# A gated recurrence on one core: loads in series, half rows first for two tiles, plain warm-up products, the end in two pieces

## What is computed

```python
for i in range(6):                       # ih: (6, 4000, 256), hh: (6, 256, 256)
    gate = ih[i][token]                  # token: 1024 integers, 49 to 31985
    state = jnp.tanh(state + jnp.matmul(state, hh[i]) * gate)
```

## Time and profile before

| what | value |
|---|---|
| median of 3 runs | 63.14 us (62.12, 63.14, 63.68) |
| profiled execution, own time | 62.04 us |
| its span, first to last instruction | 60.2 us |
| TensorE matmul busy | 52.1 us, 86% |
| VectorE busy | 40.5 us, 67% |
| ScalarE busy | 40.0 us, 66% |
| POOL busy | 34.4 us, 57% |
| DMA moved | 4.46 MB |

### The profile page before, as it was taken

How to read it: one execution, slowest core, us unless ns; L and a number is a source line. 1 busy time by engine, 2 the same in 40 slices (tenths; PEclk the granted TensorE clock), 3 DMA queues, 4 the chain that set the end, 5 groups by cost and what they waited for, 6 DMA issues and landing times.

```text
span 60.2 us, 853 instructions
## 1 busy us (share of the span) xinstructions
PE 52.1 (86%) x273; PEld 43.2 (72%) x273; DVE 40.5 (67%) x60; ACT 40.0 (66%) x69; POOL 34.4 (57%) x34
## 2 busy tenths in 40 slices
PE   0879999995887999999999999999999999999000
PEld 0679888872747689896888887888878888885000
DVE  0319974429589885874977778877779777779900
ACT  0703899503329440979999888998888988852430
POOL 4076076777624990298587876667866668700000
PEclk9999999999999999999999999999999999999975
DMA  0598688898400000000000000000000000032254
GB/s 0 12 321 271 211 280 242 222 303 222 131 16 0 0 0 0 0 0 11 0 0 0 0 0 0 0 0 5 11 5 0 0 0 0 0 144 97 107 195 154
DMA packets 5380, 4.46 MB, mean 74 GB/s; under 512 B 2186, under 2 KB 4746, under 8 KB 5376
## 3 DMA queue, kind: packets, MB, share of 16 engines
q1 hardware_dynamic: 3168, 3.41, 17.7%
q0 software_dynamic: 1152, 0.73, 4.8%
q10 hardware_dynamic: 1056, 0.27, 1.9%
HBM read 8.92 MB, written 1.05 MB: 166 GB/s over the span
## 4 chain that ended last, share of the span: by engine, by line
PE 66%; DMA 12%; issue 5%; DVE 5%; ACT 4%; POOL 3%; DVEq 0%; POOLq 0%
PE prod L443 25%; PE prod L452 12%; PE turned L427 12%; PE prod L400 9%; DMA gate<-gates_dram,row_of 8%; PE turned L465 5%; DMA last_row<-gates_dram 4%; PE turned L409 4%; POOL gate L214 3%; ACT gate L256 2%; DVE prod L349 1%; DVE pre L354 1%; DVE gp L338 1%; ACT s L267 1%; ACT s L282 1%
## 5 line engine op out<-in xcount | busy, mean ns | idle before, releaser
L230 POOL TENSOR_TENSOR sl<-s,sh 128x512 fp32r<-128x512 f32 x12 | 15.5, 1291 | 6.0 <-ACT s L282 6.0
L443 PE MATMUL prod<-sh,wr 128*128 128x512 f32 x64 | 18.8, 415 | 0.0
L400 PE MATMUL prod<-w,s 128*128 128x256 f32 x64 | 15.3, 388 | 1.3 <-ACT s L267 0.6
L349 DVE TENSOR_TENSOR prod<-prod,gate_t 128x512 f32<-128x512 f32 x16 | 11.2, 700 | 6.5 <-PE prod L452 6.5
L400 PEld LDWEIGHTS prod<-w,s 128*128 128x128 f32 x64 | 12.1, 197 | 3.1 <-issue 1.7
L443 PEld LDWEIGHTS prod<-sh,wr 128*128 128x128 f32 x64 | 10.9, 189 | 1.5
L282 ACT ACTIVATE s<-pre 128x512 f32<-128x512 f32 x16 | 9.9, 620 | 2.6 <-DVE pre L354 2.6
L354 DVE TENSOR_TENSOR pre<-prod,s 128x512 f32<-128x512 f32 x16 | 11.1, 693 | 0.6
L214 POOL DMA_INDIRECT gate<-gates_dram,row_of x8 | 8.1, 1010 | 5.6 <-issue 2.0
L452 PE MATMUL prod<-sl,wr 128*128 128x512 f32 x32 | 10.0, 395 | 0.0
L427 PE MATMUL turned<-ident,gate 128*128 128x128 f32 x64 | 9.4, 272 | 0.0
(11 more groups left out here) (20 smaller groups left out, 26.6 us busy)
## 6 DMA issues: line engine op xcount, KB each, us to landing
w<-hh_dram SPq DMA_DIRECT2D x5, 256.0 KB
s<-state_t_dram SPq DMA_DIRECT2D x4, 256.0 KB, 3.3
out_t_dram<-s SPq DMA_DIRECT2D x4, 256.0 KB, 2.0
w<-hh_dram ACTq DMA_DIRECT2D x1, 256.0 KB
gate<-gates_dram,row_of POOLq DMA_INDIRECT x8, 3.2
last_row<-gates_dram ACTq DMA_DIRECT2D x1, 6.0 KB, 2.5
tok<-token_dram SPq DMA_DIRECT2D x1, 4.0 KB, 1.7
```

Source lines behind the costliest of these rows:

```text
L230: nc.gpsimd.tensor_tensor(of_unit(sl[:, l % 2], h, c), of_unit(s, h, c), of_unit(sh[:, l % 2], h, c).bitcast(f32), ALU.subtract).then_inc( ...
L349: nc.vector.tensor_tensor(prod_bank[u][:, :], prod_bank[u][:, :], gate_t[:, u], ALU.mult).then_inc(unit_gated[u], 1)
L400: last = nc.tensor.matmul(prod[q][:, t, :], of_quarter(s, q)[:, c, t * P:(t + 1) * P], w[:, l, c, :], start=c == 0, stop=c == KC - 1)
L443: nc.tensor.matmul(prod_bank[u][:, :], wr[:, l, k, half, c * P:(c + 1) * P], of_unit(sh[:, (l - 1) % 2], h, k), start=half == 0 and k == 0 ...
```

## The change

- SP issues each load only when the one before it has landed: state 2 behind state 1, then state 3, weights 1, 2, 3, 4 and 5 in turn.
- Tiles 0 and 1 are fetched in halves of a row, through a view of the table with twice as many rows (`half_of` is twice the row). The first halves (layers 0 to 2) are gathered first and patched on VectorE; the second halves are gathered behind all other tiles, into space that ScalarE has filled with two more fills. VectorE has one patch fewer.
- The warm-up products are nine plain matmuls of 64 columns on a tile of zeros that VectorE clears, in place of five transposes of the identity.
- `gate_t` has two buffers, by the parity of the layer, and the order of ScalarE's gate copies is written out anew.
- The last tanh and the last store are cut into two pieces of 256 batch columns.

```diff
-WARM_UP = 5
...
-LATE_TILES = [0, 1]
+WARM_UP = 9
+EARLY_TILES = [0, 1]
...
+HALF = LAYERS // 2 * HIDDEN
+EARLY, REST = slice(0, HALF), slice(HALF, 2 * HALF)
...
+ACT_FILLS = [(1, 2, 1), (2, 2, 1), (1, 3, 1), (2, 3, 1), (1, 4, 2), (2, 4, 2), (1, 6, 2), (2, 6, 2), (2, 0, 2)]
+ACT_COUNT = len(ACT_FILLS) + 1
...
+    half_table = table.rearrange("v (h n) -> (v h) n", n=HALF)
...
-        gate_t = sb("gate_t", [P, UNITS, HB], f32)
+        gate_t = sb("gate_t", [P, 2, UNITS, HB], f32)
...
-                sp.wait_ge(state_in[0], 16)
+                sp.wait_ge(state_in[1], 16)
                 load_state(2)
-                sp.wait_ge(w_in[0], 16)
+                sp.wait_ge(state_in[2], 16)
                 load_state(3)
-                sp.wait_ge(state_in[1], 16)
+                sp.wait_ge(state_in[3], 16)
                 load_weights(1)
-                sp.wait_ge(state_in[2], 16)
-                load_weights(2)
-                sp.wait_ge(state_in[3], 16)
-                load_weights(3)
-                for l in range(4, LAYERS):
-                    sp.wait_ge(w_in[l - 3], 16)
+                for l in range(2, LAYERS):
+                    sp.wait_ge(w_in[l - 1], 16)
                     load_weights(l)
                 for h in range(HALVES):
                     for c in range(KC):
                         sp.wait_ge(unit_s[h * KC + c], wide_done(LAYERS - 1))
-                        sp.dma_start(out_v[h, c], of_unit(s, h, c)).then_inc(out_done, 16)
-                sp.wait_ge(out_done, 16 * UNITS)
+                        if h * KC + c < UNITS - 1:
+                            sp.dma_start(out_v[h, c], of_unit(s, h, c)).then_inc(out_done, 16)
+                        else:
+                            sp.dma_start(out_v[h, c, :, 0:QB], of_unit(s, h, c)[:, 0:QB]).then_inc(out_done, 16)
+                            sp.wait_ge(end_s, 1)
+                            sp.dma_start(out_v[h, c, :, QB:HB], of_unit(s, h, c)[:, QB:HB]).then_inc(out_done, 16)
+                sp.wait_ge(out_done, 16 * (UNITS + 1))
...
+                def gather_early(t):
+                    nc.gpsimd.indirect_dma_start(
+                        gate[:, t, EARLY], None, half_table,
+                        bass.IndirectOffsetOnAxis(half_of[:, t:t + 1].bitcast(u32), 0),
+                        bounds_check=last_half_fetched, oob_is_err=False,
+                    ).then_inc(early_in[t], 16)
+                def gather_rest(t):
+                    pool.wait_ge(filled_act, ACT_COUNT)
+                    nc.gpsimd.indirect_dma_start(
+                        gate[:, t, REST], None, half_table,
+                        bass.IndirectOffsetOnAxis(half_of[:, t:t + 1].bitcast(u32), 0),
+                        element_offset=HALF, bounds_check=last_half_fetched, oob_is_err=False,
+                    ).then_inc(gate_in[t], 16)
                 def gather(t):
-                    if t not in LATE_TILES:
-                        pool.wait_ge(filled_dve, fills_of(t, DVE_FILLS))
-                        pool.wait_ge(filled_act, fills_of(t, ACT_FILLS))
+                    pool.wait_ge(filled_dve, fills_of(t, DVE_FILLS))
+                    pool.wait_ge(filled_act, fills_of(t, ACT_FILLS))
...
+                pool.wait_ge(halves_ready, 1)
+                for t in EARLY_TILES:
+                    gather_early(t)
                 pool.wait_ge(rows_ready, 1)
-                for t in range(TILES):
+                for t in range(len(EARLY_TILES), TILES):
                     gather(t)
+                for t in EARLY_TILES:
+                    gather_rest(t)
...
-                    if l > WIDE:
-                        act.wait_ge(unit_gated[u], wide_done(l - 1))
-                    nc.scalar.copy(gate_t[:, u], turned_bank[u][:, :]).then_inc(gates_copied[u], 1)
+                    if l > WIDE + 1:
+                        act.wait_ge(unit_gated[u], wide_done(l - 2))
+                    nc.scalar.copy(gate_t[:, l % 2, u], turned_bank[u][:, :]).then_inc(gates_copied[u], 1)
...
-                    nc.scalar.activation(of_unit(s, h, c), of_unit(pre, h, c), ACT.Tanh).then_inc(unit_s[u], 1)
+                    if (l, u) != (LAYERS - 1, UNITS - 1):
+                        nc.scalar.activation(of_unit(s, h, c), of_unit(pre, h, c), ACT.Tanh).then_inc(unit_s[u], 1)
+                    else:
+                        s_u, pre_u = of_unit(s, h, c), of_unit(pre, h, c)
+                        nc.scalar.activation(s_u[:, 0:QB], pre_u[:, 0:QB], ACT.Tanh).then_inc(unit_s[u], 1)
+                        nc.scalar.activation(s_u[:, QB:HB], pre_u[:, QB:HB], ACT.Tanh).then_inc(end_s, 1)
...
+                nc.scalar.copy(gate[:, 0:len(EARLY_TILES), HALF:HALF + HIDDEN],
+                               spread[1][:, HIDDEN:2 * HIDDEN].unsqueeze(1).to_broadcast([P, len(EARLY_TILES), HIDDEN]),
+                               ).then_inc(filled_act, 1)
...
+                copy_gates(WIDE, 1, 0)
+                for l in range(WIDE, LAYERS - 1):
+                    wide_tanh(l, 0, 0)
+                    copy_gates(l, 1, 1)
+                    wide_tanh(l, 0, 1)
+                    copy_gates(l + 1, 0, 0)
+                    wide_tanh(l, 1, 0)
+                    copy_gates(l + 1, 0, 1)
+                    wide_tanh(l, 1, 1)
+                    copy_gates(l + 1, 1, 0)
+                wide_tanh(LAYERS - 1, 0, 0)
+                copy_gates(LAYERS - 1, 1, 1)
+                wide_tanh(LAYERS - 1, 0, 1)
+                wide_tanh(LAYERS - 1, 1, 0)
+                wide_tanh(LAYERS - 1, 1, 1)
...
+                nc.vector.memset(blank[:, :], 0.0).then_inc(blank_ready, 1)
...
+                nc.vector.tensor_scalar(wrap[:, :], tok_held[:, :], 0.0, 2.0 * VOCAB, ALU.is_lt, ALU.mult).then_inc(index_step, 1)
...
-                nc.vector.tensor_tensor(row_of[:, :], tok_held[:, :], wrap[:, :], ALU.add).then_inc(rows_ready, 1)
+                nc.vector.scalar_tensor_tensor(half_of[:, :], tok_held[:, :], 2.0, wrap[:, :], ALU.mult, ALU.add).then_inc(halves_ready, 1)
+                dve.wait_ge(halves_ready, 1)
+                nc.vector.tensor_scalar(row_of[:, :], half_of[:, :], 0.5, None, ALU.mult).then_inc(rows_ready, 1)
...
-                def patch(i, t, count):
-                    for late in range(t, t + count):
-                        dve.wait_ge(gate_in[late], 16)
-                    nc.vector.copy_predicated(filled(i, t, count),
-                                              is_last[:, t:t + count].unsqueeze(2).to_broadcast([P, count, PIECE * HIDDEN]),
-                                              filling(i, count)).then_inc(patched, 1)
+                def patch(t):
+                    dve.wait_ge(early_in[t], 16)
+                    nc.vector.copy_predicated(gate[:, t, 0:PIECE * HIDDEN], is_last[:, t:t + 1].to_broadcast([P, PIECE * HIDDEN]),
+                                              spread[0]).then_inc(patched, 1)
+                def patch_rest():
+                    dve.wait_ge(filled_act, ACT_COUNT)
+                    tiles = slice(0, len(EARLY_TILES))
+                    nc.vector.copy_predicated(gate[:, tiles, PIECE * HIDDEN:HALF],
+                                              is_last[:, :].unsqueeze(2).to_broadcast([P, len(EARLY_TILES), HIDDEN]),
+                                              spread[1][:, 0:HIDDEN].unsqueeze(1).to_broadcast([P, len(EARLY_TILES), HIDDEN]),
+                                              ).then_inc(patched, 1)
...
-                patch(0, 0, 1)
+                patch(0)
                 for i, t, count in DVE_FILLS[3:]:
                     fill(i, t, count)
-                patch(0, 1, 1)
+                patch(1)
                 gating(0)
                 gating(1)
                 sum_up(0)
-                dve.wait_ge(filled_act, len(ACT_FILLS))
-                patch(1, 0, 2)
+                patch_rest()
                 gating(2)
                 sum_up(1)
                 sum_up(2)
-                patch(2, 0, 2)
...
+                    if h == 0 and l < LAYERS // 2:
+                        pe.wait_ge(patched, len(EARLY_TILES) + 1)
+                    elif h == 0:
+                        for t in EARLY_TILES:
+                            pe.wait_ge(gate_in[t], 16)
...
+                pe.wait_ge(blank_ready, 1)
+                for _ in range(WARM_UP):
+                    nc.tensor.matmul(turned[0][:, 0, 0:P // 2], blank[:, :], blank[:, 0:P // 2], start=True, stop=True)
                 pe.wait_ge(ident_ready, 1)
-                for _ in range(WARM_UP):
-                    nc.tensor.transpose(turned[0][:, 0, 0:P], ident[:, :], ident[:, :])
```

More of the change, by code:

```diff
@@ L83, in recurrent_cells @@
         row_of = sb("row_of", [P, TILES], i32)
-        is_last = sb("is_last", [P, len(LATE_TILES)], i32)
+        half_of = sb("half_of", [P, TILES], i32)
+        is_last = sb("is_last", [P, len(EARLY_TILES)], i32)
+        blank = sb("blank", [P, P], f32)
         last_row = sb("last_row", [P, LAYERS, KC], f32)
```

(24 more changed lines are left out.)

3 lines of the change are left out of this document (removed).

## The result

| | median us | all runs |
|---|---|---|
| before | 62.84 | 62.12 to 63.68 (4 runs) |
| changed | 67.0 | 65.71, 66.25, 67.76, 69.38 |
| ratio | 1.058 | 95% interval 1.034 to 1.083 |

The change makes the kernel slower. The medians lie 4.2 us apart; the ratio is formed from the fast runs alone (65.71 and 66.25 against 62.12 and 62.55), and by these the loss is 3.6 us. The profiled execution of the changed kernel took 69.38 us (span 67.6), and TensorE's clock dipped in it for 3.3 us: its mean clock is 0.971. The runs of 65.71 and 66.25 have a mean clock of 0.99; a dip of that length alone would bring it to 0.974 (an estimate), so they had none like it.

What follows compares the result with a forecast made beforehand. Gathers hold the kernel up to 18.40 us, then TensorE's fixed order; the start of plain(7) is the mark. +0.8 for serial loads and -0.3 at the end make 62.04 into 62.5, plus half the distance to the median: 63.1, range 60.8 to 65.2.

Steps and rivals of the forecast that it cites:

- the second rival: SP's serial loads cost more, 3.15 to 3.34 us each beside gathers: slower, 64.3 to 65.1 us; chance 0.22.
- the price of a load in series: SP's queue: 2.7 us for each of four loads beside gathers, 2.1 for each of the last three.
- C: Average time of SP's seven serial loads, forecast at 2.44 us; break-even against the profiled execution at 2.37.
- its 63.6: Total in us by the skill's rule, which prices a lone load at 2.6; the forecast kept the rows instead.
- The mechanism: ScalarE: tanh(3) stands behind the rounding of weights 5, so the last plain product, plain(7), starts 0.8 us later.
- The formula 62.04 + 7C - 16.6: Total time from the profiled 62.04 us, the delay of plain(7) by seven serial loads, and 0.3 saved at the end.
- The third rival: TensorE's clock falls in the idle time before plain(7), costing 2.5 us: 65.0 us; chance 0.06.
- the hole before plain(7): TensorE standing idle some 2 us before the last plain product, waiting for tanh(3).
- The warm-up: TensorE's head: earlier start worth nothing while serial loads set the mark, at worst costs nothing; 1.3 to 1.5 us possible.
- The end: Last tanh and store cut in two: 0.3 us faster, between 0 and 0.5.
- Gathers: Gathers fall from 4.54 towards 3.2 us, up to 1.3 won at plain(5), then lost at plain(7).
- Half rows and gate buffers: Half-row fetches save 1.9 us on DVE, which does not end last; doubled gate_t removes a nonbinding wait: nothing.

Runs made afterwards that it cites:

- a_oldwarm: The changed kernel with the five transposes of the identity as warm-up again; 67.75 us, ratio 1.086 to the kernel before.
- b_serial: The kernel before with only SP's seven later loads put in series; 68.41 us against 62.24.
- b_warm: The kernel before with only the warm-up changed to nine plain products of zeros; 63.73 us, ratio 1.024.
- b_end: The kernel before with only the last tanh and last store cut in two; 62.9 us, ratio 1.011.
- a_old3: The changed kernel with loads, warm-up and end of before, leaving half rows, fills and gate buffers; 62.33 us against 62.12, ratio 1.006.
- b_warm_ones: The kernel before with nine plain warm-up products on a tile of ones; 63.75 us, ratio 1.026.
- a_warm4: The changed kernel with SP's waits of before and four plain products of zeros as warm-up; 62.64 us, ratio 1.010.
- b_ones4: The kernel before with four plain products of ones, 128 columns, as warm-up; 62.2 us against 62.12.

## Why the prediction was wrong

The forecast was no clear change, 63.1 us, between 60.8 and 65.2; measured were 67.0 in the median and 65.98 in the mean of the two quickest runs. The direction was that of the second rival (0.22), and the size lay beyond even its upper end of 65.1.

- **The step that failed is the price of a load in series.** The forecast took 2.1 for a nearly lone load, by the stores, and 2.7 beside gathers. Measured: 2.7 and 3.2 in a_oldwarm, 2.6 to 2.8 for a quite lone one. The average C was 3.0, not 2.44. Two wrong choices lie in it: a store of the same size was taken as the nearest row, though it goes the other way; and the one row of loads beside gathers (3.34, the state 2 load) was used as an upper bound and averaged with the store's, when it was close to the value. The rule of the Trainium skill ("DMA: Bandwidth & Descriptors", section "Anatomy of one DMA"), set aside for the rows, was right for the lone load to 0.2 us (2.60 against 2.63 to 2.77), and its 63.6 fell short mainly because the four loads beside the gathers took 3.2.
- **The mechanism was right.** The formula 62.04 + 7C - 16.6, with the C = 3.0 of a_oldwarm, gives 66.4, and with the end at +0.05 instead of -0.3 it is 66.8; its profiled execution took 66.85. In the changed kernel C was 3.07 and state 2 was issued 0.3 us later than forecast; with the 1.9 of the dip this makes 69.5, and 69.38 were measured. Its two quickest runs would need a C of 2.9 and no dip (an estimate; they have no profile). From landing to plain(7) it was 1.32 in the changed kernel against the 1.33 of the forecast. Moving the roundings brought plain(7) from 29.27 back to 23.26 with the loads unchanged, which shows that ScalarE's queue carries the loss and not traffic or TensorE's own need for the weights.
- **The third rival came true on top.** The clock fell 0.4 to 0.5 us behind the hole before plain(7) in the profiled executions of the changed kernel and of b_serial, and cost 1.9 us in the changed kernel; in a_oldwarm it did not fall. It was treated as an alternative with 0.06, when it hangs on the same hole as the forecast: the profiled executions with the roundings moved, without the hole, have no dip ahead of the end.
- **The warm-up was mis-sized.** "At worst it costs nothing" was wrong by 1.5 us in b_warm. A float32 product is two instructions here; the rows before had eight L400 instructions for the four products of a step, and were not read for it. In the changed kernel it cost nothing, for the reason given: the loads did not wait for it.
- **The end** was forecast at -0.3 and wins nothing: 0.15 paid and 0.1 back in the profile, 1% slower when run alone in b_end, and no gain from taking it out in a_old3.
- **Gathers** did land sooner with the loads in series: the one issued at 11.64 landed at 16.18 before, and in b_serial gating 2 ran at 15.32 without waiting for it. In the changed kernel plain(5) came later all the same, at 20.30 instead of 18.40: tanh(1) stood behind the rounding of weights 2, which landed at 19.0 and not 16.8. The gain of this term was lost earlier than the forecast said.
- **Half rows and gate buffers**: nothing, as forecast; a_old3 is 0.6% over before.

Open: why the changed kernel spreads from 65.71 to 69.38 us by more than the dip, why b_end is slower by more than its tail shows, whether ones raise the clock earlier than zeros, and why the moved sums win with half rows and not clearly without them.

## What to carry to other kernels

A chain of transfers, each waiting for the last one, costs the whole way from issue to landing each time; price it with a lone transfer of the same direction and size, measured if no row shows one, and multiply by its length. Then look in every engine's queue for what stands behind a wait on such a transfer: here the roundings could wait without harm, and the tanhs behind them could not. When an experiment moves work on another engine along with it, as with POOL's subtractions here, look there too before the rest of the loss is put down to the change. Where a step is forecast to leave TensorE idle, the fall of TensorE's clock belongs to that case and is no separate one.

## What the runs showed of the hardware

- A lone load of 256 KB took 2.63 to 2.77 us from issue to landing, one of 128 KB 1.99 to 2.15, a store of 256 KB 2.0 to 2.1, a store of 128 KB 1.9.
- TensorE's granted clock fell to the lower level in two profiled executions after it had stood idle for 2.5 and 2.7 us and worked again for 0.4 and 0.5 us (changed kernel, b_serial), and stayed there for 3.3 us; after 2.53 us of idleness in a_oldwarm it did not fall. In b_warm_ones TensorE had waited 1.9 us up to 16.69, then did one turn, and the clock fell near 17.3 and stayed low longest; the stretch (clock is the third number from the end):

```profile
17.30:24.10 6.80, 6.17 (x18) 5.00 (x18) 3.73 (x5) 2.93 (x6) 2.53 (x2) 0.50 0.06 14
```

- A plain float32 product of 64 columns is two instructions of 0.23 us each at the head of the kernel: eighteen took 4.1 us. Eight of 64 columns took 1.97 (a_warm4) and eight of 128 columns 2.07 (b_ones4), so the number of columns hardly counts at this size.
